# The first state of each channel group: four scaled copies by ScalarE in place of four products by VectorE, in a decoder layer

## What is computed

```python
x = silu(causal_conv(u) + conv_b)                # u: 2048 channels, 512 tokens, batch of 2
dt, B, C = split(x @ Wx.T)                       # each with an RMS norm; N = 16 states
delta = softplus(dt @ Wdt.T + dt_bias)
def step(state, (d_t, B_t, C_t, u_t)):           # over the 512 tokens
    state = exp(d_t[..., None] * A) * state + (d_t * u_t)[..., None] * B_t[:, None, :]
    y_t = einsum('bdn,bn->bd', state, C_t)
y = (ys + u * D_param) * silu(gate)
out = y @ W_out.T
```

## Time and profile before

| | |
|---|---|
| median of 3 runs | 1704.55 us (1702.2 to 1712.32) |
| the profiled execution | 1702.31 us, its span 1700.5 us |
| mean granted TensorE clock | 0.922 |
| TensorE busy with matmuls | 1392.4 us (82%) |
| VectorE | 1346.4 us (79%) |
| ScalarE | 908.5 us (53%) |
| GpSimd | 971.1 us (57%) |

### The profile page before, as it was taken

How to read it: one execution, slowest core, us unless ns; L and a number is a source line. 1 busy time by engine, 2 the same in 40 slices (tenths; PEclk the granted TensorE clock), 3 DMA queues, 4 the chain that set the end, 5 groups by cost and what they waited for, 6 DMA issues and landing times. The chain is left out here.

```text
span 1700.5 us, 17655 instructions
## 1 busy us (share of the span) xinstructions
PE 1392.4 (82%) x5384; PEld 712.7 (42%) x5384; DVE 1346.4 (79%) x1642; ACT 908.5 (53%) x1314; POOL 971.1 (57%) x794
## 2 busy tenths in 40 slices
PE   6998676778878987668788778788889985999788
PEld 3443343444444444344444444444434442444333
DVE  6586699998898899999998989989148465777784
ACT  1211658657667755857767657655143122556640
POOL 0000778888787877989898898887100001333540
PEclk9999788889999988958999989999999996999899
DMA  7596232443442432433682682664482104589204
GB/s 269 200 346 251 90 126 95 167 141 104 155 155 99 166 105 94 148 94 118 229 257 90 230 259 81 240 205 155 173 308 100 50 25 138 128 179 216 59 0 173
DMA packets 155466, 264.36 MB, mean 155 GB/s; under 512 B 76560, under 2 KB 94096, under 8 KB 149552
## 3 DMA queue, kind: packets, MB, share of 16 engines
q1 hardware_dynamic: 151056, 236.27, 42.8%
q10 hardware_dynamic: 4320, 27.00, 4.4%
HBM read 207.60 MB, written 38.60 MB: 145 GB/s over the span
## 5 line engine op out<-in xcount | busy, mean ns | idle before, releaser
L1031 DVE TENSOR_TENSOR_SCAN hbuf<-decay,hbuf 128x512 f32<-128x512 f32 x512 | 610.8, 1209 | 50.0 <-ACT decay L757 50.0
L757 ACT ACTIVATE decay<-delta,chan_sb 128x512 f32<-128x512 f32 x512 | 348.2, 687 | 319.5 <-DVE hbuf L1031 318.2
L577 PE MATMUL turn<-ident,hbuf 128*128 128x128 f32 x2048 | 348.0, 301 | 207.0 <-DVE hbuf L1031 162.2
L577 PEld LDWEIGHTS turn<-ident,hbuf 128*128 128x128 f32 x2048 | 262.2, 154 | 486.2 <-DVE hbuf L1031 242.4
L1045 DVE SCALAR_TENSOR_TENSOR acc<-turn,pn,acc 128x512 f32<-128x512 f32 x360 | 262.1, 728 | 30.1 <-PE turn L577 28.6
L868 POOL TENSOR_TENSOR hbuf<-du,sx 128x512 f32<-128x512 f32 x172 | 213.0, 1272 | 1.9 <-DMA sx<-bt_scratch 1.9
L868 POOL TENSOR_TENSOR hbuf<-wout,sx 128x512 f32<-128x512 f32 x172 | 213.4, 1275 | 0.4 <-POOL wout L878 0.2
L889 POOL TENSOR_TENSOR acc<-acc,part 128x512 f32<-128x512 f32 x120 | 153.3, 1278 | 60.1 <-ACT part L767 58.2
L1731 PE MATMUL bank<-codes,wout 128*128 128x512 bf16 (+1 forms) x704 | 153.9, 382 | 1.0 <-PEq L1144 1.0
L559 PE MATMUL bank_g<-wout,codes 128*128 128x512 f32 x256 | 137.8, 625 | 0.8 <-DVE wout L968 0.8
L491 PE MATMUL bank_u<-wout 128*128 128x512 f32 x224 | 112.7, 623 | 3.1 <-DMA wout<-in_wu 2.2
(11 more groups left out here) (210 smaller groups left out, 2096.3 us busy)
## 6 DMA issues: line engine op xcount, KB each, us to landing
wout<-in_woutT SPq DMA_DIRECT2D x48, 512.0 KB, 4.4
sx<-bt_scratch SPq DMA_DIRECT2D x86, 256.0 KB, 3.7
codes<-in_wg SPq DMA_DIRECT2D x8, 2048.0 KB, 8.8
ubuf<-u_scratch SPq DMA_DIRECT2D x16, 1024.0 KB, 5.9
wout<-in_w_gate SPq DMA_DIRECT2D x26, 512.0 KB, 4.7
wout<-in_w_up SPq DMA_DIRECT2D x26, 512.0 KB, 4.0
raw_d<-in_w_down ACTq DMA_DIRECT2D x8, 1376.0 KB, 6.8
b_more<-bt_scratch SPq DMA_DIRECT2D x42, 256.0 KB, 3.5
```

The lines of the kernel that those rows point to most:

```text
L577: last = pe.transpose(turn[t % 2][:, j * P:j * P + P], hbuf[:, s % 4, j, t * P:t * P + P], ident[:, :])
L757: act.activation(decay_bank[q % 2][:, :], delta[:, G % 2, j, :], ACT.Exp, scale=a_col(GD * (G % GROUPS) + j, n)).then_inc(dA_done, 1)
L1031: dve.tensor_tensor_scan(h, decay_bank[q % 2][:, :], h, 0.0, ALU.mult, ALU.add).then_inc(scan_done, 1)
```

## The change

At n = 0 ScalarE writes all four tiles of `acc` from the `turn` banks by a Copy activation with the column of C as scale (`first_state`), and VectorE makes none of them. Tiles 0 and 1 stand on ScalarE behind decays 2 and 3 of step n = 1, tiles 2 and 3 behind decays 0 and 1 of step n = 2. They count on a semaphore of their own, `first_done`; whoever waited for VectorE's product of n = 0 waits for it: TensorE's transposes for t = 2, 3 of n = 0 and for t = 0, 1 of n = 1, VectorE's sums of n = 1, and GpSimd's first addition of a group. `mac` counts without n = 0. Apart from this the memset of the padding of `code_d` goes from GpSimd to VectorE, behind the three memsets, and those who wait for constants wait for one more.

```diff
--- before.py
+++ after.py
@@ -179,6 +179,7 @@
         scan_done = sem("scan_done")
         turned = sem("turned")
         mac_done = sem("mac_done")
+        first_done = sem("first_done")
         part_done = sem("part_done")
         part_added = sem("part_added")
         gate_mm = sem("gate_mm")
@@ -255,7 +256,7 @@
 
         def mac(s, tt):
             G, n = s // N, s % N
-            return (TT * N - N + 1) * G + (TT + ZT * (n - 1) if n else 0) + tt + 1
+            return ZT * ((N - 1) * G + n - 1) + tt + 1
 
         def moved_count(s):
             return (N - 1) * (s // N) + s % N
@@ -565,8 +566,12 @@
                 s = N * G + n
                 if t == 0:
                     pe.wait_ge(scan_done, GD * (s + 1))
-                if t >= 2:
+                if t >= 2 and n == 0:
+                    pe.wait_ge(first_done, TT * G + t - 1)
+                elif t >= 2:
                     pe.wait_ge(mac_done, mac(s, t - 2))
+                elif n == 1:
+                    pe.wait_ge(first_done, TT * G + t + 3)
                 elif s >= 1 and moved(s - 1, t + 2):
                     pe.wait_ge(part_done, moved_count(s - 1))
                 elif s >= 1:
@@ -767,6 +772,14 @@
                 act.activation(part[:, k % 2, :], turn[ZT % 2][:, :], ACT.Copy,
                                scale=pn[:, G // GROUPS, ZT, c:c + 1]).then_inc(part_done, 1)
 
+            def first_state(s, t):
+                G = s // N
+                act.wait_ge(turned, bank_turn(G, 0, t))
+                if G >= 2:
+                    act.wait_ge(y_sum, GD * (G - 1))
+                act.activation(acc[:, G % 2, t, :], turn[t % 2][:, :], ACT.Copy,
+                               scale=pn[:, G // GROUPS, t, R + N:R + N + 1]).then_inc(first_done, 1)
+
             def gate_copy(G, j):
                 act.wait_ge(gate_mm, GD * G + j + 1)
                 if G >= 1:
@@ -813,6 +826,9 @@
                     s = N * G + n
                     for j in range(2, GD):
                         decay(s, j)
+                    if n == 1:
+                        for t in range(2):
+                            first_state(s - 1, t)
                     quant(2 * s)
                     if n == 0 and G >= 1:
                         for j in gate_copies(G - 1, N):
@@ -827,7 +843,10 @@
                     if s + 1 < STEPS:
                         for j in range(2):
                             decay(s + 1, j)
-                    if s >= 1 and moved(s - 1, ZT):
+                    if n == 1:
+                        for t in range(2, TT):
+                            first_state(s - 1, t)
+                    elif s >= 1 and moved(s - 1, ZT):
                         scaled_state(s - 1)
                     quant(2 * s + 1)
                     if n == 0 and G >= 1:
@@ -882,7 +901,7 @@
                 k = moved_count(s)
                 pool.wait_ge(part_done, k)
                 if s % N == 1:
-                    pool.wait_ge(mac_done, mac(s - 1, ZT))
+                    pool.wait_ge(first_done, TT * (s // N + 1))
                 else:
                     pool.wait_ge(part_added, k - 1)
                 a = acc[:, s // N % 2, ZT, :]
@@ -1031,19 +1050,19 @@
                 dve.tensor_tensor_scan(h, decay_bank[q % 2][:, :], h, 0.0, ALU.mult, ALU.add).then_inc(scan_done, 1)
 
             def add_states(s, t):
-                if moved(s, t):
+                if s % N == 0 or moved(s, t):
                     return
                 G, n = s // N, s % N
                 dve.wait_ge(turned, bank_turn(G, n, t))
                 a = acc[:, G % 2, t, :]
                 c = R + N + n
                 state = turn[t % 2][:, :]
-                if n == 0:
-                    dve.tensor_scalar(a, state, pn[:, G // GROUPS, t, c:c + 1], None, ALU.mult).then_inc(mac_done, 1)
+                if n == 1:
+                    dve.wait_ge(first_done, TT * G + t + 1)
                 else:
                     dve.wait_ge(mac_done, mac(s - 1, t))
-                    dve.scalar_tensor_tensor(a, state, pn[:, G // GROUPS, t, c:c + 1], a, ALU.mult, ALU.add)\
-                        .then_inc(mac_done, 1)
+                dve.scalar_tensor_tensor(a, state, pn[:, G // GROUPS, t, c:c + 1], a, ALU.mult, ALU.add)\
+                    .then_inc(mac_done, 1)
 
             def weight_max(u):
                 n = unit_rows(u)
@@ -1632,7 +1651,6 @@
         wd_step = sem("wd_step")
         wd_code = sem("wd_code")
         wd_plain = sem("wd_plain")
-        pad_made = sem("pad_made")
         wd_turned = sem("wd_turned")
         gate_mm = sem("gate2_mm")
         up_mm = sem("up_mm")
@@ -1690,7 +1708,7 @@
             def turn_wd(t):
                 sp.wait_ge(wd_plain, NP * (t + 1))
                 if t == 0:
-                    sp.wait_ge(pad_made, 1)
+                    sp.wait_ge(const, 4)
                 sp.dma_start(wdT[:, 0:OC, t * P:t * P + P], code_d[:, :], transpose=True).then_inc(wd_turned, 16)
 
             def load_x2(i):
@@ -1811,7 +1829,7 @@
 
             for t in range(2):
                 load_wd(t)
-            act.wait_ge(const, 3)
+            act.wait_ge(const, 4)
             for k in range(SLOTS + 1):
                 if k < SLOTS:
                     silu(k)
@@ -1857,7 +1875,6 @@
                 v = hid[0:r, bass.ds(c, 1), L:2 * L]
                 pool.tensor_tensor(v, v, ih_row[0:r, L:2 * L].unsqueeze(1), ALU.mult).then_inc(q_scaled[1], 1)
 
-            pool.memset(code_d[:, INTER:OC * P], 0.0).then_inc(pad_made, 1)
             for k in range(SLOTS):
                 multiply(k)
             pool.wait_ge(ih_kept, 2)
@@ -1901,7 +1918,8 @@
             dve.memset(rnd[:, 0:1], ROUND).then_inc(const, 1)
             dve.memset(rnd[:, 1:2], -ROUND).then_inc(const, 1)
             dve.memset(peak[:, :], 0.0).then_inc(const, 1)
-            dve.wait_ge(const, 3)
+            dve.memset(code_d[:, INTER:OC * P], 0.0).then_inc(const, 1)
+            dve.wait_ge(const, 4)
             for k in range(SLOTS + 2):
                 if k < SLOTS:
                     scale_products(k)
```

## The result

The changed kernel takes 1716.61 us (median of 12 runs, 1710.27 to 1720.09) against 1703.36 us of the kernel before on the same chips (12 runs): the ratio is 1.007, 95% interval 1.005 to 1.009. The forecast was 1716. The profiled execution has a span of 1714.8 us, 14.3 more than before.

What follows compares the result with a forecast made beforehand. Late bank release by ScalarE's copies at group starts, with slow TensorE restarts, was to outweigh VectorE's relief; eight group terms summed to +11.8 us, 1716.4 from the median, put at 1716, range 1702 to 1725.

Steps and rivals of the forecast that it cites:

- The chain: Third group's start: copies behind the decays free banks late, TensorE restarts slowly, VectorE waits for the bank; +2.4 us.
- the fourth: Fourth group's start, double products of the x projection: +3.9 us with first product slow, second fast; +2.0 at full speed.
- The new wait of VectorE for transposes: Sign at each group's start from the second on: VectorE waits 1 to 4 us before its first sum of n = 2.
- The first group: First group's start, no Silu ahead and TensorE not held up: -1.2 us, with no new wait for transposes.
- One sign of being wrong: The prediction is wrong if TensorE's transposes after the restart at a group's start take 0.6 us.
- The eighth, 0.1: Eighth group's start: only 0.1 us lost, since weights of the output projection arrive late there anyhow.
- The seventh, 2.15: Seventh group's start: TensorE restarts after the first copy, two transpose sets and double products take 4.50 us; +2.15 us.
- The third: Third group's start: +2.4 us, or +0.2 with TensorE at full speed and +3.0 if slow to the end.
- fast bound of 1704: Lower case of the forecast time: TensorE fast in every group, group starts summing to +2.6 us.
- the slow one: Upper case of the forecast time: TensorE slow longer, group starts summing to +18.0 us, 1722.6 us.
- VectorE's relief of 20.8 us: Rival for the state scan: the work taken off VectorE counts in full, 20.8 us faster, 1684 us; chance 0.06.
- A fast TensorE: Rival: TensorE stays fast or later waits make up the lag; -4 to +3 us, 1701 to 1708; chance 0.22.
- More slow stretches than forecast: Rival: TensorE stays slow longer and new idle time brings more slow stretches; +18 us and more, 1722 to 1728; chance 0.15.

Runs made afterwards that it cites:

- e2: Kernel before, VectorE still making all four first products but late, behind its third and fourth scans of step n = 1; ratio to before 1.0131, +22 us.
- e9: Kernel before with ScalarE copying only tiles 2 and 3, ahead of the code step, which moves behind the next decays too; ratio to before 0.9964.
- e3: Changed kernel plus 28 identity transposes on TensorE between tiles 1 and 2 of the first state, groups 2 to 8; ratio to before 1.0038.
- e11: Changed kernel with 28 added identity transposes a group from the second on, but 44 in the third; its one execution took 1708.7 us.
- e1: Kernel before with only the padding's memset moved to VectorE; ratio to before 1.0007.

## Why the prediction was right

**The bound.** Read from the place and not from the shares: VectorE works 19 us less in the scan and idles 34 us more. e2 and e9 are the two sides of it: lateness without a copy on ScalarE loses 22 us, two copies on ScalarE without lateness win 6.

**The chain.** Its steps came as written in the third group: copy behind the two decays, TensorE restarting 0.05 us later and slowly, VectorE's scan hardly earlier (3.08 us behind the scan after the Silu against 3.55), then the wait for the bank. What only e3 and e11 show is the size of the slow clock: of 15.3 us in groups 2 to 8 about 7.6 go when TensorE is kept busy. Of the 7.7 left, 2.4 stand in the eighth group, where the added transposes were in the way, and 1.4 in the third are taken by e11; what remains, 3.9, is the order alone, above all the fourth group's 2.0.

**The signs.** The new wait of VectorE for transposes is there in every group from the second on, 1.2 to 4.2 us. VectorE's busy time fell by 18.9 us and ScalarE's rose by 17.4, not by 23 and 21: an engine's busy time counts overlapping stretches once (it is no sum of records, as the text ahead of the prediction has it), so of the removed 23.3 us only the 20.8 that the prediction itself gives could come off; the other 1.9 are not traced. The first group, for which no such wait was expected, has one of 0.95 us and is 1.0 us shorter all the same. One sign of being wrong did show in part. The transposes after the restart were to be slow; in the second, fourth and sixth group the first four took 0.66 us, after 2.56, 3.40 and 2.72 us of waiting, and the slow stretch began only with the product behind them, as TensorE's timeline of the second group shows:

```profile
327.02 0.66 PE L582 MATMUL turn<-ident,hbuf 128*128 128x128 f32 x4 [2.56 <-ACT acc L780]
327.52 1.86 PE L492 MATMUL bank_u<-wout 128*128 128x512 f32 x2
```

So TensorE did lose time at the lower clock in each of these groups, but not always from the place where the prediction had it.

**The terms.** The first six groups came within 0.6 us each. In the fourth the first product was forecast slow (3.4) and the second fast (1.7); both were slow in part, 2.55 and 2.15 from start to start. Two terms were mis-sized. The eighth, 0.1, measured 1.8: I let TensorE restart at full speed there, but it waited 0.92 us for the copy and its transposes and products were slow, as TensorE's timeline of the changed kernel shows.

```profile
1102.01 1.97 PE L582 MATMUL turn<-ident,hbuf 128*128 128x128 f32 x8 [0.92 <-ACT acc L780]
1103.77 1.92 PE L607 MATMUL bank_u<-wout 128*128 128x512 f32 x2
1105.48 1.19 PE L607 MATMUL bank_s<-wout 128*128 128x512 f32 x2
```

The seventh, 2.15, measured 3.2, since both double products were slow and not only the first. The third was 0.5 too high, since the clock rose sooner than before. The sum was 2.5 us low, and the 2.3 us that later steps lost were given back behind the scan. That the time came within 1 us of the forecast is in part luck: the terms missed both ways, the 11.8 us were put on a median of 1704.55 where twelve runs of the kernel before give 1703.36, so that the difference is 13.3, and the time between the jumps moves by 2 us from one execution to the next. The range has a slip as well: its fast bound of 1704 is the profiled execution's 1702.31 plus 2.6, while the slow one is counted from the median, from which the fast one would be 1707.2.

**The rivals.** VectorE's relief of 20.8 us came only to the extent that e9 has it, 1.2 us a group. The rule of the Trainium skill (Perfetto Trace Analysis, Identifying the Most-Contended Engine) is to optimize the engine with the highest occupancy first. The trace agrees on the engine, VectorE, busy 91% of the stretch, but taking this work from it gained nothing: in the seven groups behind a Silu half of the work had stood where VectorE waits anyway, and it had given the banks back. A fast TensorE would have left +2.6 us in the jumps by the forecast; e3 and e11 together come near it except in the eighth group, and the fourth's +2.0 is in both forecast and runs. More slow stretches than forecast didn't come: the mean granted clock is 0.92 in both. The memset cost nothing that e1 could show.

## What to carry to other kernels

Before work is taken from the busiest engine, look at what that engine does at the very place: work that fills its idle time is free, and it may be what gives a buffer back early. Of a moved step ask who waits for the buffer that it frees, and put it on an in-order engine ahead of what nobody waits for. Then move only the part that lies on the path: here two products of four, with a code step moved out of their way.

## What the runs showed of the hardware

In the third group TensorE was slow at its restart after 2.49 us of waiting (e3, 1.12 us for four transposes) and not after 0.73 us (e11, 0.66 us), and about half of what the late release cost lay in such restarts (7.6 of 15.3 us): 44 useless transposes of 4.97 us in all took 1.4 us off the group's delay.

The length of the wait alone does not decide it. In the kernel before, TensorE waited 3.79 us at another place, and its transposes and the product behind them ran at full speed (granted clock 1.00):

```profile
493.00 0.66 PE L577 MATMUL turn<-ident,hbuf 128*128 128x128 f32 x4 [3.79 <-DVE hbuf L1031]
493.49 1.02 PE L491 MATMUL bank_u<-wout 128*128 128x512 f32 x2
```

In the third group 4.32 us ended in 1.12 us. The granted clock can also still be 1.00 inside a wait and be low only behind the restart, as in the windows of the changed kernel's third group above and in e3's. What decides between the two is not shown by any run here, so the clock at a restart has to be read from the trace and not from the wait.
